# Another order of the calls in front of the loop of a fused attention and feed-forward kernel

## The reference

```python
def _layernorm(x, axis=-1, eps=1e-05):
    return (x - mean) / jnp.sqrt(var + eps)

def reference(t, W_qkv, b_qkv, w_gate, w_up, w_down):     # t: (16, 1024, 256) float32
    def attn(t):                                          # W_qkv: (768, 256)
        qkv = jnp.einsum('bnd,ed->bne', t, W_qkv) + b_qkv
        Q, K, V = qkv[:, :, :256], qkv[:, :, 256:512], qkv[:, :, 512:]
        scores = jnp.einsum('bqd,bkd->bqk', Q, K) / sqrt(256)
        return jnp.einsum('bqk,bkv->bqv', jax.nn.softmax(scores, axis=-1), V)
    def ffn(x):                                           # int32 weights, hidden size 768
        gate = jnp.einsum('bsd,hd->bsh', x, w_gate / 127)
        up = jnp.einsum('bsd,hd->bsh', x, w_up / 127)
        return jnp.einsum('bsh,dh->bsd', jax.nn.silu(gate) * up, w_down / 127)
    x = t
    x = x + _layernorm(attn(_layernorm(x)))
    x = x + _layernorm(ffn(_layernorm(x)))
    return x
```

## Time and profile before

| | before |
|---|---|
| median of 3 runs | 1376.56 us |
| profiled execution | 1376.6 us |
| its span, first to last instruction | 1374.7 us |
| PE busy | 1352.9 us (98%) |
| DVE busy | 897.3 us (65%) |
| ACT busy | 877.5 us (64%) |
| POOL busy | 825.2 us (60%) |
| granted TensorE clock | 0.999 |

### The profile page before, as it was taken

The page is one execution under the profiler, slowest core; times in us unless marked ns, Lnnn a source line. Parts: engine busy times, 40 slices in busy tenths (PEclk is TensorE's granted clock), DMA queues, the critical chain, the costliest instruction groups (busy, mean ns, idle before and its releaser), DMA issues.

```text
span 1374.7 us, 22429 instructions
## 1 busy us (share of the span) xinstructions
PE 1352.9 (98%) x7437; PEld 728.8 (53%) x7437; DVE 897.3 (65%) x2160; ACT 877.5 (64%) x1373; POOL 825.2 (60%) x1002
## 2 busy tenths in 40 slices
PE   8999999999999999999999999999999999999997
PEld 4444555554555555555554555545555555555554
DVE  6786666666757667666766657667566666656555
ACT  4757475766756667575675767567566775756644
POOL 2768375573837658476484756748376583745545
PEclk9999999999999999999999999999999999999999
DMA  7996382654727466382753836447383663716411
GB/s 199 188 185 149 68 163 78 116 130 84 147 85 135 104 112 143 77 163 68 137 132 70 161 77 123 123 95 144 78 151 88 123 133 80 141 55 114 94 40 55
DMA packets 437176, 158.29 MB, mean 115 GB/s; under 512 B 418113, under 2 KB 420417, under 8 KB 437058
## 3 DMA queue, kind: packets, MB, share of 16 engines
q1 hardware_dynamic: 436272, 156.03, 54.4%
q10 hardware_dynamic: 786, 0.79, 0.2%
HBM read 36.70 MB, written 16.78 MB: 39 GB/s over the span
## 4 chain that ended last, share of the span: by engine, by line
PE 91%; DVE 3%; SPq 2%; DMA 2%; issue 1%; POOL 1%; ACT 0%; ACTq 0%; POOLq 0%
PE S L710 90%; DMA yTl<-yl 1%; SPq L245 1%; PE S L729 1%; DVE mxs L613 1%; DVE S L642 0%; SPq L226 0%; DVE st L651 0%; POOL rs L293 0%; SPq L251 0%; DMA xTl<-xl 0%; POOL Pl L338 0%; DVE xl L320 0%; POOL yl L365 0%; DVE X L664 0%
## 5 line engine op out<-in xcount | busy, mean ns | idle before, releaser
L438 ACT ACTIVATE P<-S,nmx,sc 128x1024 f32<-128x1024 f32 x128 | 153.6, 1200 | 283.1 <-DVE nmx L617 283.1
L613 DVE TENSOR_REDUCE mxs<-S 128x1 f32<-128x1024 f32 x128 | 156.1, 1220 | 124.7 <-PE S L710 124.4
L679 DVE SCALAR_TENSOR_TENSOR hf<-S,sc,hf 128x512 f32<-128x512 f32 x192 | 141.9, 746 | 140.6 <-ACT hf L473 134.4
L338 POOL TENSOR_TENSOR Pl<-P,Ph 128x1024 f16<-128x1024 f32 x96 | 205.9, 2145 | 33.9 <-issue 26.4
L710 PE MATMUL S<-xTh,zTh 128*128 128x512 f16 x512 | 194.1, 379 | 4.2 <-ACT P L438 2.2
L710 PE MATMUL S<-PTh,xl 128*128 128x512 f16 x512 | 194.0, 379 | 0.0
L710 PE MATMUL S<-xTl,zTh 128*128 128x512 f16 x512 | 194.0, 379 | 0.0
L710 PE MATMUL S<-xTh,zTl 128*128 128x512 f16 x512 | 194.0, 379 | 0.0
L710 PE MATMUL S<-PTl,xh 128*128 128x512 f16 x512 | 194.0, 379 | 0.0
L710 PE MATMUL S<-PTh,xh 128*128 128x512 f16 x512 | 194.0, 379 | 0.0
L289 POOL TENSOR_SCALAR rs<-mv,sc 128x2 f32<-128x2 f32 (+1 forms) x96 | 35.2, 367 | 231.5 <-DVE mv L655 191.8
(11 more groups left out here) (115 smaller groups left out, 2476.1 us busy)
## 6 DMA issues: line engine op xcount, KB each, us to landing
xs<-in_L_attn_t SPq DMA_DIRECT2D x32, 512.0 KB, 5.3
X<-in_L_attn_t SPq DMA_DIRECT2D x32, 512.0 KB, 4.4
out_x<-X SPq DMA_DIRECT2D x64, 256.0 KB, 2.9
PTh<-Ph SPq DMA_TRANSPOSE x128, 3.2
PTl<-Pl SPq DMA_TRANSPOSE x128, 3.2
hTh<-in_L_attn_W_qkv ACTq DMA_DIRECT2D x1, 768.0 KB, 7.2
hTl<-in_L_ffn_w_gate SPq DMA_DIRECT2D x1, 768.0 KB, 7.4
hTh<-in_L_ffn_w_up SPq DMA_DIRECT2D x1, 768.0 KB, 9.1
```

What stands on the lines that cost most here:

```text
L338: p.engine.tensor_tensor(out=Pl[:, m % 3, :], in0=P[:, m % 2, :], in1=Ph[:, m % 3, :], op=ALU.subtract).then_inc(pl_vector if i in PL_ON_V ...
L438: a.engine.activation(P[:, m % 2, :], ps[:, bank:bank + 2, :].rearrange("p a n -> p (a n)"), ACT.Exp, bias=nmx[:, c:c + 1], scale=sS, accu ...
L613: v.engine.tensor_reduce(mxs[:, c:c + 1], ps[:, bank:bank + 2, :].rearrange("p a n -> p (a n)"), axis=AX.X, op=ALU.max, negate=True).then_ ...
L679: v.engine.scalar_tensor_tensor(out=hf[:, n % 3, :], in0=ps[:, bank + 1, :], scalar=sc2[:, 4:5], in1=hf[:, n % 3, :], op0=ALU.mult, op1=AL ...
```

## The change

On SP, POOL, ACT and DVE the calls in front of the loop stand in another order. No call is added or left out, no argument changes, and the loop, the tail and PE's list are as they were. The diff, cut to the places spoken of:

```diff
@@ SyncE
             turn_x(s, 0, 1, 0)
+            load_x(s, 1, 0)
             turn_x(s, 0, 1, 1)
-            load_x(s, 1, 0)
             load_x(s, 1, 1)
+            load_ffn(s, 2)
             load_ffn(s, 0)
-            load_ffn(s, 1)
-            load_ffn(s, 2)
             turn_v(s, 0)
             turn_v(s, 1)
+            load_ffn(s, 1)
...
@@ GpSimd
             p_low(p, 0, 0)
+            x_low(p, 1, 0)
             x_hat_pool(p, 1, 1)
-            x_low(p, 1, 0)
             p_low(p, 0, 2)
             p_low(p, 0, 3)
...
@@ ScalarE
             x_hat(a, 0, 1)
+            A_high(a)
             x_high(a, 0, 1)
-            A_high(a)
             V_high(a)
...
             o_high(a, 0, 1, 1)
-            p_high(a, 1, 3)
             o_high(a, 0, 1, 0)
             x_high(a, 2, 0)
+            x_high(a, 2, 1)
+            exp(a, 1, 3, 2)
             exp(a, 1, 4, 0)
+            p_high(a, 1, 3)
             p_high(a, 1, 4)
             y_hat(a, 0, 0, 0)
-            x_high(a, 2, 1)
             y_hat(a, 0, 0, 1)
             y_high(a, 0, 0)
             exp(a, 1, 5, 2)
...
@@ VectorE
             scale_A(v)
-            x_low(v, 0, 1)
             A_low(v)
             attention_scales(v)
+            x_low(v, 0, 1)
             V_low(v)
             z_float(v, 0, 0, 0)
             z_low(v, 0, 0)
             x_stats(v, 1, 0)
+            x_stats(v, 1, 1)
             row_max(v, 0, 0, 4)
-            x_stats(v, 1, 1)
+            z_float(v, 0, 1, 2)
             row_max(v, 0, 1, 6)
-            z_float(v, 0, 1, 2)
             row_max(v, 0, 2, 0)
+            z_low(v, 0, 1)
             p_low(v, 0, 1)
-            z_low(v, 0, 1)
             row_max(v, 0, 3, 2)
```

More of the change, by code:

```diff
@@ L861, in _ @@
             turn_p(s, 0, 1, 0)
-            turn_p(s, 0, 1, 1)
             turn_x(s, 1, 0, 0)
             turn_x(s, 1, 0, 1)
+            turn_p(s, 0, 1, 1)
+            load_x(s, 2, 0)
             turn_p(s, 0, 2, 0)
@@ L1039, in _ @@
             p_low(p, 1, 0)
+            z_low(p, 1, 1)
             x_norm(p, 2, 0)
             x_norm(p, 2, 1)
-            z_low(p, 1, 1)
-            x_hat_pool(p, 2, 1)
             y_norm(p, 0, 0)
             p_low(p, 1, 2)
-            p_low(p, 1, 3)
+            x_hat_pool(p, 2, 1)
             x1_norm(p, 0, 0)
             x_low(p, 2, 0)
+            x_low(p, 2, 1)
+            p_low(p, 1, 3)
+            y_low(p, 0, 0)
             y_norm(p, 0, 1)
-            y_low(p, 0, 0)
             p_low(p, 1, 5)
-            x_low(p, 2, 1)
+            p_low(p, 1, 6)
             x1_norm(p, 0, 1)
-            p_low(p, 1, 6)
-            p_low(p, 1, 7)
             y_low(p, 0, 1)
@@ L1061, in _ @@
             h_low(p, 0, 0, 4)
-            z_low(p, 2, 1)
-            x_norm(p, 3, 0)
             h_low(p, 0, 1, 0)
             h_low(p, 0, 1, 1)
+            p_low(p, 1, 7)
+            x_norm(p, 3, 0)
+            d_norm(p, 0, 0, 1)
             h_low(p, 0, 1, 3)
+            d_norm(p, 0, 0, 0)
+            z_low(p, 2, 1)
+            p_low(p, 2, 0)
             x_norm(p, 3, 1)
             h_low(p, 0, 1, 4)
-            d_norm(p, 0, 0, 0)
-            d_norm(p, 0, 0, 1)
-            p_low(p, 2, 0)
             for b in range(1, 13):
@@ L1231, in _ @@
             exp(a, 1, 5, 2)
+            exp(a, 1, 6, 0)
             p_high(a, 1, 5)
-            exp(a, 1, 6, 0)
             p_high(a, 1, 6)
             exp(a, 1, 7, 2)
+            silu(a, 0, 0, 0, 6)
             p_high(a, 1, 7)
-            silu(a, 0, 0, 0, 6)
+            z_high(a, 2, 0, 0)
             y_hat(a, 0, 1, 0)
             y_hat(a, 0, 1, 1)
-            z_high(a, 2, 0, 0)
+            silu(a, 0, 0, 1, 2)
             y_high(a, 0, 1)
             h_high(a, 0, 0, 0)
-            silu(a, 0, 0, 1, 2)
+            h_high(a, 0, 0, 1)
             silu(a, 0, 0, 2, 6)
-            h_high(a, 0, 0, 1)
+            h_high(a, 0, 0, 2)
             silu(a, 0, 0, 3, 0)
-            h_high(a, 0, 0, 2)
             silu(a, 0, 0, 4, 2)
             h_high(a, 0, 0, 3)
+            h_high(a, 0, 0, 4)
             z_high(a, 2, 1, 6)
-            h_high(a, 0, 0, 4)
             silu(a, 0, 0, 5, 0)
@@ L1261, in _ @@
             silu(a, 0, 1, 4, 6)
+            silu(a, 0, 1, 5, 0)
             h_high(a, 0, 1, 3)
-            silu(a, 0, 1, 5, 0)
             h_high(a, 0, 1, 4)
+            h_high(a, 0, 1, 5)
+            o_high(a, 1, 0, 1)
+            exp(a, 2, 0, 0)
             x_hat(a, 3, 0)
-            h_high(a, 0, 1, 5)
+            p_high(a, 2, 0)
+            o_high(a, 1, 0, 0)
             x_hat(a, 3, 1)
-            exp(a, 2, 0, 0)
-            p_high(a, 2, 0)
-            o_high(a, 1, 0, 1)
+            add_bias(a, 0, 0, 1)
             add_bias(a, 0, 0, 0)
-            o_high(a, 1, 0, 0)
-            add_bias(a, 0, 0, 1)
             exp(a, 2, 1, 2)
@@ L1522, in _ @@
             row_max(v, 0, 7, 4)
+            x_stats(v, 2, 0)
+            row_max(v, 1, 0, 0)
             ffn_low(v, 0)
-            row_inverse(v, 0, 1)
-            row_max(v, 1, 0, 0)
             ffn_low(v, 1)
@@ L1529, in _ @@
             o_low(v, 0, 0, 0)
-            x_stats(v, 2, 0)
+            x_stats(v, 2, 1)
             row_max(v, 1, 1, 2)
-            x_stats(v, 2, 1)
             z_float(v, 1, 1, 0)
+            row_inverse(v, 0, 0)
+            y_scale(v, 0, 0, 0)
+            row_inverse(v, 0, 1)
             p_low(v, 1, 1)
-            y_scale(v, 0, 0, 0)
-            y_scale(v, 0, 0, 1)
             y_stats(v, 0, 0, 0)
             row_max(v, 1, 2, 0)
+            y_scale(v, 0, 0, 1)
             y_stats(v, 0, 0, 1)
+            x1_add(v, 0, 0, 0)
+            x1_add(v, 0, 0, 1)
+            o_low(v, 0, 1, 1)
             row_max(v, 1, 3, 2)
-            x1_add(v, 0, 0, 0)
+            o_low(v, 0, 1, 0)
+            row_max(v, 1, 4, 0)
             row_inverse(v, 1, 0)
[L1543 to L1546, removed]
             y_scale(v, 0, 1, 0)
@@ L1581, in _ @@
             d_add(v, 0, 0, 0)
+            h_low(v, 0, 1, 5)
+            o_low(v, 1, 0, 1)
             d_add(v, 0, 0, 1)
-            o_low(v, 1, 0, 1)
+            x_stats(v, 3, 1)
             for b in range(1, 13):
```

95 lines of the change are left out of this document (45 added, 50 removed).

## The result

| | before | changed |
|---|---|---|
| median | 1376.53 us (8 runs, 1375.64 to 1377.24) | 1380.41 us (8 runs, 1379.34 to 1381.82) |
| profiled execution | 1376.6 us | 1379.81 us |
| its span | 1374.7 us | 1378.0 us |
| PE busy | 1352.9 us | 1355.0 us |
| mean granted clock | 0.999 | 0.996 |

The account below looks back on a forecast made before the run. PE, busy for 98% of the span, bounds the kernel, so only its waits ahead of 130 us count. The terms +2.6 - 2.0 + 0.2 - 0.9 - 0.4 + 0.2 = -0.3 gave 1376.3 us, range 1373.0 to 1379.5.

Parts of the forecast that it names:

- A: Start of project_z(0,1) on PE, after the low transpose of x lands: from 21.74 to 24.3, +2.6 us.
- B: Start of score(0,4) on PE: 13.3 us behind A with z_low(0,1) earlier on DVE, -2.0 us.
- C: Start of score(0,7) on PE: 14.0 us behind B, turn_max waiting 0.2 for exp(0,5), +0.2 us.
- rival 4: x_hat_pool on POOL keeps its 4.2 us: 1378.3 us, chance 0.07.
- D: Start of score(1,7) on PE: 50.7 us behind C, still waiting for ACT's exp(1,5), -0.9 us.
- E: Start of gate_up(0,0,0) on PE, after the low y lands: 4.15 us behind D, -0.4 us.
- F: Start of gate_up(0,1,0) on PE: 16.1 us behind E, no wait there, +0.2 us.
- Rival 1: At project_z(0,1), low transpose lands at 26.0 behind load_x(1,0), load_x(1,1) late too: 1379.4 us, chance 0.16.
- Rivals 2 and 3: 2: cheap start, end pays more, 1373.5 us, chance 0.18. 3: loop entry late, 1377.8 with 1.5, chance 0.11.

Follow-up runs that it names:

- e6: Changed kernel with only SP's move undone (load_x(1,0) back behind the low transpose); 1376.72 us, 0.9997.
- e1: Changed kernel plus 40 matmuls of 256 columns on the identity, result unread, in PE's wait ahead of project_z(0,1); 1377.02 us, 1.0006.
- e3: Kernel before with only the change's three moves at the start (ACT's A_high, DVE's x_low(0,1), SP's load_x(1,0)); 1382.29 us, 1.005.
- e2: Changed kernel with its three moves at the start undone (ACT's A_high, DVE's x_low(0,1), SP's load_x(1,0)); 1374.38 us, 0.9991.
- e8: Kernel before with only DVE's early moves (x_stats(1,1), z_float(0,1) and z_low(0,1) earlier); 1376.21 us, 0.9998.
- e7: e2 with x_high(2,1) on ACT moved behind p_high(1,6), x_low(2,1) on POOL behind x1_norm(0,1), their transposes later on SP; 1374.50 us, 0.9986.
- e9: e7 with y_hat(0,0,0) moved ahead of exp(1,4) on ACT; 1375.17 us, 0.9988.
- e4: e2 with SP's move alone left in (load_x(1,0) ahead of the low transpose); 1379.35 us, 1.0022.
- e11: e4 plus 24 filler matmuls in PE's wait at project_z(0,1); 1379.65 us, 1.0018.
- e5: Changed kernel with only ACT's swap undone (A_high back behind x_high(0,1)); 1378.07 us, 1.0012.

## Why the prediction was wrong

**A failed**, twice. Its start was forecast at 24.3 and was 24.88: the load ahead of the transpose held SP for 1.23 us and not 0.6, and the landing took 5.1, not 4.8. The prediction took the 4.8 of the same transpose before, and set a longer landing aside since no row showed a transpose behind a load. The trace of before has such places, which its rows left out. SP's queue before, at 50 us, and the landing of the transpose there (the same 256 KB):

```profile
50.54 1.45 SPq L215 DMA_DIRECT2D xs<-in_L_attn_t  x2
52.03 1.24 SPq L245 DMA_TRANSPOSE PTh<-Ph  x1
...
DMA to landing us min/median/max: 6.2/6.2/6.2
```

It is 6.2 again at 110.30 and 6.1 at 278.69, each directly behind two loads. Taken for A, 6.2 gives 25.7 and a sum of +1.1 us. The reading of the 4.8 was wrong too. It was put down to two loads issued behind the transpose, but e6 has those two behind it just the same and lands in 3.2. The high transpose directly ahead isn't enough for it either: low transposes of P and y in the same place behind another (before, 37.34 and 119.47) land in 3.4. What made the 4.8 stays open. All this is the small part, +0.6. The large one is that the step priced only the length of the wait. It had PE idle for some 4.2 us at A and took no further cost from it, and behind such a wait PE comes back at 1.2 GHz. The trace has +2.27 us for it, e1 takes this away (2.60 us from A to `score(0, 0)`), and e3 shows the same 0.50 behind a wait as long, for 1.9 us more. The bounds of A, +1.0 to +4.2, left this out too, so the range did. With the +2.27 and the +0.6 the forecast's own sum would be -0.3 + 2.9 = +2.6 us, or 1379.2, and what the profiled execution shows is 1379.8.

**B held.** 13.33 us behind A without the slow matmuls, for 13.3; in e2 13.35. Both statistics of block 1 fitted in ahead of the first row maximum. But e8 shows that the -2.0 isn't worth 2.0 by itself: without the moves behind it 1.1 goes into the wait of `turn_max`.

**C held**: 14.13 for 14.0. `x_hat_pool` took 4 x 0.56 us, so rival 4 is out.

**D nearly held**: 50.98 for 50.7, and the wait for ACT of 1.23 us was forecast as 1.2 seen. That ACT comes next when DVE is out of the path was right; e7 and e9 show that behind ACT come PE's own scores and the transposes of P.

**E failed in small**: 4.45 for 4.15, so the gain of 0.4 was 0.07. The path to it was right, and the wait is for DMA.

**F held**: 15.99 for 16.1, without a wait at F. The new wait of 0.35 just behind it, at `gate_up(0, 1, 1)`, wasn't seen in the walk.

Together, against the terms added to the marks of before: +0.54 at A, +2.27 of slow matmuls, +0.01 at B, +0.13 at C, +0.25 at D, +0.33 at E, -0.12 at F: 3.41 us, the whole distance from 122.62 to 126.03.

**The rivals.** Rival 1 gave 1379.4 and comes close to the time, by another mechanism: it had the landing at 26.0 and a late load holding B, and neither is in the trace (24.88; B 13.33 behind A without the slow matmuls). It was the right place. That the transpose waits behind the load has something in it: issued directly behind a load it took 5.1, 5.0, 5.1, 5.8 and 6.2 (changed, e1, e3, e4, e11), with 2 us between the end of the load's issue and its own 3.4 (e5), and without one ahead 3.2 (e6) or 4.8 (before). The Trainium skill, DMA: Bandwidth & Descriptors, section on queues, rings and completion order, has descriptors of a ring taken in ring order; these runs agree in direction, and 1.8 to 3.0 us over the 3.2 is what the load ahead cost here. Not one of them held it until 26.0. Rivals 2 and 3 didn't occur: the loop's idle time is unchanged to 0.1 us.

Left open: why the medians of the changed kernel and of e1 are 3.4 us apart where the traces explain 1.7 to 2.3, and what parts e4's runs. A fall behind the last wait, worth 1.66 us where it was seen, may have a share in both: the two longest runs of the changed kernel (1381.67 and 1381.82) have the lowest mean clock, 0.995, but no trace of them shows where it fell.

## What to carry over

Price a wait of TensorE in two parts: its length, and the risk that 3 to 5 us of the work behind it run at half the rate, which cost 1.7 to 2.3 us wherever these traces show it. The two waits of almost 5 us had it both times, waits of 1.7 to 2.9 us in some executions and not in others. Look for it at every wait up to the end of the program, the last one too. A reordering that moves a small piece of work off one path and adds a few us to the one that PE is waiting for can lose more than the whole of what it wins elsewhere; undoing just that piece kept the rest, and made the better kernel (e2, 0.9991, and e7, 0.9986 with 0.9977 to 0.9995). And follow a gain to the next wait of the same engine before it is counted: of 1.9 us at B 0.75 was left at C in e8. And before a cost is left out because no row shows it, look through the whole trace of before: the price of a transpose behind a load stood there, at 52 us.

## What the runs showed of the hardware

- Behind PE's wait of 4.94 us the granted clock was 0.50, and the next twelve matmuls took 4.86 us, for 2.60 at 1.00. Behind 4.97 us (e3) they took 4.50. Waits of 2.63 and 2.67 us had a fall in the profiled executions of e6 and e5 (4.29 us), one of 2.94 (e4) hadn't; one of 2.19 had it in e8, and not before.
- Behind the last wait, of 1.72 us in all fourteen profiled executions, the clock fell in three (e4, e5, e6), and the 48 matmuls there took 7.09 us for 5.42.
- 40 matmuls of 256 columns on the identity in the wait at A kept the clock at 1.00, and A came 0.68 us later.
- How long a transpose of 256 KB took to land went with what was issued ahead of it on the queue: 5.0 to 6.2 us directly behind a load of 512 KB or two, 3.2 to 3.4 with 0.8 us or more between the two issues (e6, e5). Directly behind another transpose it was 3.4 at some places of before (37.34, 43.61, 119.47) and 4.2 to 4.8 at others (16.93, 47.74, 49.12). The issue of such a load took 0.58 us (e4, e5, e11), 1.23 and 1.26 (changed, e3) or 1.90 (e1); what sets that wasn't tried.
- From `gate_up(0, 1, 1)` to the last wait, with the same code in all kernels, the profiled executions took 1236.8 to 1239.3 us.
